# First batch's opening and last batch's end in another order: ranking, weight splits, maxima, and the split of the heads

## The reference

```python
def _L0_ffn_ref(x, w_router, w_block):
    k = max(1, int(L * CAPACITY_RATIO))            # 768 of 1024
    scores = jnp.einsum('bld,d->bl', x, w_router)
    _, top_idx = jax.lax.top_k(scores, k)
    selected = jnp.take_along_axis(x, top_idx[:, :, None], axis=1)
    processed = jax.nn.gelu(jnp.einsum('bkd,de->bke', selected, w_block))
    out = x.at[batch_idx, top_idx].set(processed)

def _L0_attn_ref(hidden_states, Wq, Wk_down, Wv_down, q_to_latent, v_up, Wout):
    Q = (hidden_states @ Wq.T).reshape(b, t, h, d)     # 16 heads of 32
    latent_k = hidden_states @ Wk_down.T               # 64 wide
    latent_v = hidden_states @ Wv_down.T
    q_lat = jnp.einsum('bthd,hdl->bthl', Q, q_to_latent)
    logits = jnp.einsum('bthl,bsl->bhts', q_lat, latent_k) / math.sqrt(l)
    # causal mask, softmax
    ctx_lat = jnp.einsum('bhts,bsl->bhtl', attn, latent_v)
    heads = jnp.einsum('bhtl,hld->bthd', ctx_lat, v_up)
    out = heads.reshape(b, t, h * d) @ Wout.T

x = x + 0.5 * _L0_ffn_ref(_layernorm(x), ...)
x = x + _L0_attn_ref(_layernorm(x), ...)
x = x + 0.5 * _L0_ffn_ref(_layernorm(x), ...)
```

## Time and profile before

| | us |
|---|---|
| median of three executions | 2589.89 |
| the profiled execution, its time | 2591.08 |
| the profiled execution, its span | 2589.4 |
| PE busy | 2348.7 (91%) |
| DVE busy | 1719.9 (66%) |
| ACT busy | 1181.7 (46%) |
| POOL busy | 395.1 (15%) |
| mean granted PE clock | 0.965 of full |

### The profile page before, as it was taken

The page is one execution under the profiler, slowest core; times in us unless marked ns, Lnnn a source line. Parts: engine busy times, 40 slices in busy tenths (PEclk is TensorE's granted clock), DMA queues, the critical chain, the costliest instruction groups (busy, mean ns, idle before and its releaser), DMA issues.

```text
span 2589.4 us, 53629 instructions
## 1 busy us (share of the span) xinstructions
PE 2348.7 (91%) x21888; PEld 1457.0 (56%) x21888; DVE 1719.9 (66%) x4806; ACT 1181.7 (46%) x2071; POOL 395.1 (15%) x510
## 2 busy tenths in 40 slices
PE   6769999899989998899998999989999899998976
PEld 4534567445664556645575546654476545674445
DVE  4658656785667756686566865678656785567735
ACT  3325543464425643356433554445543455424542
POOL 0101211112101121111111101111111112101121
PEclk9879999999999999999999999999999899999998
DMA  3200021100201002010111101210021100301000
GB/s 122 98 2 2 2 85 47 66 2 8 92 34 66 3 18 82 33 67 2 35 64 50 51 2 66 66 66 3 2 83 49 66 2 2 98 1 67 2 1 33
DMA packets 70034, 106.20 MB, mean 41 GB/s; under 512 B 3104, under 2 KB 33312, under 8 KB 67744
## 3 DMA queue, kind: packets, MB, share of 16 engines
q1 hardware_dynamic: 69792, 102.77, 11.6%
HBM read 64.49 MB, written 37.75 MB: 39 GB/s over the span
## 4 chain that ended last, share of the span: by engine, by line
PE 69%; DVE 12%; issue 10%; ACT 6%; POOL 2%; DMA 0%; DVEq 0%; POOLq 0%; ACTq 0%
PE psum L722 25%; PE psum L735 18%; PE psum L841 9%; PE psum L848 7%; PE psum L738 4%; DVE psum L973 4%; ACT pr L703 4%; PE psum L764 3%; PE psum L749 3%; DVE part L971 2%; DVE junk L923 1%; POOL rstd L596 1%; DVE junk L921 1%; DVE qk L960 1%; DVE nt_l L909 1%
## 5 line engine op out<-in xcount | busy, mean ns | idle before, releaser
L703 ACT ACTIVATE pr<-psum 128x512 f32<-128x512 f32 x1152 | 617.6, 597 | 621.3 <-PE psum L738 621.1
L735 PE MATMUL psum<-qk,qk 32*128 32x512 f32 (+3 forms) x4608 | 511.4, 369 | 97.8 <-ACT pr L703 38.9
L973 DVE CUSTOM_DVE_ANT_0 psum<-psum,mask_b 128x512 f32<-128x512 f32 (+3 forms) x1024 | 473.1, 522 | 166.6 <-PE psum L749 165.1
L735 PEld LDWEIGHTS psum<-qk,qk 32*128 32x128 f32 x4608 | 320.6, 186 | 402.9 <-ACT pr L703 123.0
L749 PE MATMUL psum<-qk,qk 32*128 32x512 f32 (+3 forms) x4608 | 514.1, 373 | 29.1 <-DVE part L971 19.6
L971 DVE TENSOR_REDUCE part<-psum 128x1 f32<-128x512 f32 x512 | 325.2, 681 | 71.7 <-PE psum L749 69.9
L749 PEld LDWEIGHTS psum<-qk,qk 32*128 32x128 f32 x4608 | 312.7, 189 | 57.5 <-DVE part L971 26.1
L614 POOL TENSOR_SCALAR_AFFINE_SELECT pr<-pr 128x512 f32<-128x512 f32 x256 | 158.0, 635 | 1056.6 <-ACT pr L703 1056.6
L841 PE MATMUL psum<-pr,v_sb 128*32 128x512 f32 (+3 forms) x3072 | 312.4, 502 | 1.6 <-ACT acc_sb L622 1.6
L848 PE MATMUL psum<-pr,ones 128*32 128x512 f32 (+3 forms) x3072 | 306.1, 493 | 0.0
L643 ACT ACTIVATE norm<-x,nmr,rstd 128x512 f32<-128x512 f32 x192 | 152.4, 810 | 193.4 <-DVE nmr L903 193.4
(11 more groups left out here) (115 smaller groups left out, 3411.4 us busy)
## 6 DMA issues: line engine op xcount, KB each, us to landing
x<-x_dram SPq DMA_DIRECT2D x16, 1024.0 KB, 6.8
spill_x<-x SPq DMA_DIRECT2D x16, 1024.0 KB, 5.2
x<-spill_x SPq DMA_DIRECT2D x16, 1024.0 KB, 7.7
out_dram<-x SPq DMA_DIRECT2D x16, 1024.0 KB, 5.1
w_h<-scratch_o SPq DMA_DIRECT2D x28, 256.0 KB, 3.1
w_l<-scratch_o SPq DMA_DIRECT2D x28, 256.0 KB, 3.3
w_h<-scratch_q SPq DMA_DIRECT2D x6, 1024.0 KB, 4.9
w_l<-scratch_q SPq DMA_DIRECT2D x6, 1024.0 KB, 6.9
```

Source lines behind the costliest of these rows:

```text
L703: nc.scalar.activation(pr_of(b, g, u)[:, 2 * p + place, :], bank(e, place), ACT.Exp, scale=SCALE).then_inc(exp_ready, 1)
L735: eng.matmul(o, (k_h, k_h, k_l)[t][own, P * j:P * (j + 1)], (q_h, q_l, q_h)[t][own, queries], start=(t == 0 and at == 0), stop=False, skip ...
L973: m = nc.vector.tensor_tensor_reduce(scores, scores, mask_b[:, BANK - w:BANK], 1.0, FAR, ALU.add, ALU.max, top_of)
```

## The change

In the first batch, `opening` replaces `front(0)`, `project(0, None)` and the maxima units 5 to 8 behind it. The first score product stands behind transposes 4 and 5; the splits 2, 3, 4 follow the second score's copy, and SCOL follows them; the first four layers stand in the list together with the ranking, then RF and all GX, then the other layers with the additions; split 5 comes ahead of the third addition. K of group 0 directly follows LAT. Maxima unit 7 stands ahead of the second LAT, and the others each stand ahead of one or two projections. All nine units of group 0 of the first batch take their banks from ring H.

In the last batch, `closing` replaces the `HS` list, `back(7)` and `ending(7)`. The heads of groups 0 to 2 are split inside group 3 (units 2 to 7), under waits of their own; those of group 3 when each half is ready, the second half of the tokens first. O, norms, transposes and scores run with the second half first. Two layers instead of four come before the ranking, and six behind it. Each half of the result is written in two pieces.

```diff
-    def front(b):
+    def opening():
...
         for i in range(NT):
-            out += [("T", 0, b, i)] + ([("NO", 0, b, i + 2)] if i + 2 < NT else [])
-            out += [("SC", 0, b, i // TC)] if i % TC == TC - 1 else []
-            out += [("WS", 1)] if i == TC else []
+            out += [("T", 0, 0, i)] + ([("NO", 0, 0, i + 2)] if i + 2 < NT else [])
+            out += [("SC", 0, 0, 0), ("WS", 1)] if i == 5 else []
+        out += [("SC", 0, 0, 1), ("WS", 2), ("WS", 3), ("WS", 4), ("SCOL", 0, 0)]
+        for i in range(TC):
+            out += layer(0, 0, i) + [("RT", 0, 0, 2 * i), ("RT", 0, 0, 2 * i + 1)]
+        out += [("RF", 0, 0)] + [("GX", 0, 0, i) for i in range(NT)]
+        out += layer(0, 0, 4) + layer(0, 0, 5) + summed(0, 0) + summed(0, 1) + [("WS", 5)]
+        out += layer(0, 0, 6) + summed(0, 2) + summed(0, 3) + scales(1, 0, 0) + layer(0, 0, 7) + [("NO", 1, 0, 0), ("NO", 1, 0, 1)]
+        after = [summed(0, 4), summed(0, 5), summed(0, 6), summed(0, 7) + scales(1, 0, 1)]
+        for i in range(TC):
+            out += [("T", 1, 0, i)] + ([("NO", 1, 0, i + 2)] if i + 2 < TC else []) + after[i]
+        out += [("LAT", 0, 0), ("XS", 0, 0), ("NO", 1, 0, 4), ("NO", 1, 0, 5), ("K", 0, 0, 0)]
+        out += [("Q", 0, 0, 0), ("T", 1, 0, 4), ("NO", 1, 0, 6), ("T", 1, 0, 5), ("NO", 1, 0, 7)]
+        out += [("Q", 0, 1, 0), ("T", 1, 0, 6), ("T", 1, 0, 7)] + maxima(0, 0, 7) + [("LAT", 0, 1), ("XS", 0, 1)]
+        out += [("XL", 1, 0), ("XL", 1, 1), ("K", 0, 0, 1), ("Q", 0, 0, 1)]
+        beside = [[("Q", 0, 1, 1)], [("K", 0, 1, 0), ("K", 0, 1, 1)], [("V", 0, 0), ("V", 0, 1)], [("Q", 0, 2, 0)],
+                  [("Q", 0, 2, 1)], [("Q", 0, 3, 0)], [("Q", 0, 3, 1)], [("V", 0, 2), ("V", 0, 3), ("V", 0, 4)]]
+        for u, rest in zip((0, 1, 2, 3, 4, 5, 6, 8), beside):
+            out += maxima(0, 0, u) + rest + sum([gathered(0, 0, c) for c in range(NC) if LAST[c] == u], [])
+            out += turned(0, 0, 1) if u == 8 else []
+        out += [("V", 0, 5), ("V", 0, 6), ("V", 0, 7), ("K", 0, 2, 0), ("K", 0, 2, 1)] + turned(0, 0, 0)
+        return out + [("K", 0, 3, 0), ("K", 0, 3, 1)]
...
-        if b + 1 == B:
-            out += layer(1, b, 6) + layer(1, b, 7)
+        return out
+
+    def closing(b, left):
+        out = left[0] + [("HS", b, NQ - 1, 1)] + left[1] + left[2] + left[3] + [("HS", b, NQ - 1, 0)]
+
+        def added(i):
+            return [("O", b, i)] + stats(2, b, i)
+
+        def turn(i):
+            after = (i + 2) % NT
+            return [("T", 2, b, i)] + ([("NO", 2, b, after)] if i % TC < 2 else [])
+
+        for i in range(TC, NT):
+            out += added(i)
+        out += scales(2, b, 1) + [("NO", 2, b, 4), ("NO", 2, b, 5)]
+        for i in range(TC):
+            out += added(i) + turn(TC + i)
+        out += scales(2, b, 0) + [("SC", 1, b, 1), ("NO", 2, b, 0), ("NO", 2, b, 1)] + layer(1, b, 4)
+        for i in range(TC):
+            out += turn(i)
+        out += [("SC", 1, b, 0)] + layer(1, b, 5) + [("SCOL", 1, b)] + [("RT", 1, b, i) for i in range(NT)] + [("RF", 1, b)]
+        order = (4, 5, 6, 7, 0, 1, 2, 3)
+        out += [("GX", 1, b, i) for i in order]
+        for i in (6, 7, 0, 1, 2, 3):
+            out += layer(1, b, i)
+        for i in order:
+            out += [("CB", 1, b, i)] + ([("OUT", b, i // TC)] if i % TC == TC - 1 else [])
         return out
...
+        else:
+            for n, (g, c) in enumerate((g, 1 - c) for g in range(NQ - 1) for c in range(NC)):
+                groups[NQ - 1][2 * n + 5] += [("HS", b, g, c)]
...
-            early = k == "MX" and e[2] == 0 and e[3] <= 4
+            early = k == "MX" and e[2] == 0 and (e[3] <= 4 or e[1] == 0)
...
+                    if b + 1 == B:
+                        sp.wait_ge(x1_ready, x1_nth["CB", 1, b, TC * c + 1])
+                        eng.dma_start(out[b, rows(c), :].rearrange("(i p) e -> p i e", p=P)[:, 0:2, :],
+                                      x1[:, TC * c:TC * c + 2, :]).then_inc(x_out[c], 16)
...
-                    act.wait_ge(heads_ready, nth["HE", b, NQ - 1, 0])
-                    act.wait_ge(q_done, nth["Q", min(b + 1, B - 1), NQ - 1, c])
+                    if b + 1 < B:
+                        act.wait_ge(heads_ready, nth["HE", b, NQ - 1, 0])
+                        act.wait_ge(q_done, nth["Q", b + 1, NQ - 1, c])
+                    else:
+                        act.wait_ge(heads_ready, nth["HE", b, g, c])
+                        act.wait_ge(s_done, nth["S", b, 1, UNITS - 1, 1])
```

More of the change, by code:

```diff
@@ L128, in summed @@
         return [("CB", 0, b, i)] + stats(1, b, i)
+    def opening():
+        out = []
+        for c in range(NC):
+            for i in range(TC * c, TC * (c + 1)):
+                out += stats(0, 0, i)
+            out += scales(0, 0, c)
+        out += [("WS", 0), ("NO", 0, 0, 0), ("NO", 0, 0, 1)]
+        for i in range(NT):
+            out += [("T", 0, 0, i)] + ([("NO", 0, 0, i + 2)] if i + 2 < NT else [])
[20 more added lines that the diff above has]
+        return out + [("K", 0, 3, 0), ("K", 0, 3, 1)]
@@ L130, in project @@
     def project(b, left):
[L134 to L137, removed]
+        out = [("G", 0, b, 0), ("G", 0, b, 1)]
         out += layer(0, b, 2) + layer(0, b, 3) + summed(b, 0) + summed(b, 1)
-        out += layer(0, b, 4) + summed(b, 2) + summed(b, 3) + scales(1, b, 0) + ([] if b else [("WS", 5)])
+        out += layer(0, b, 4) + summed(b, 2) + summed(b, 3) + scales(1, b, 0)
@@ L143, in project @@
         for i in range(TC):
[L144 removed]
+            out += [("T", 1, b, i)] + ([("NO", 1, b, i + 2)] if i + 2 < TC else []) + left[i] + after[i]
         out += [("LAT", b, 0), ("XS", b, 0), ("NO", 1, b, 4), ("NO", 1, b, 5)]
@@ L216, in more @@
         def more(kind, *rest):
-            return kind(b + 1, 0, *rest) if b + 1 < B else []
+            return kind(b + 1, 0, *rest)
         def turn(i):
@@ L242, in ending @@
         return out
-    sched = [("XL", 0, 0), ("XL", 0, 1)] + front(0) + project(0, None)
-    for u in range(5, UNITS):
-        sched += maxima(0, 0, u) + sum([gathered(0, 0, c) + turned(0, 0, c) for c in range(NC) if LAST[c] == u], [])
+    sched = [("XL", 0, 0), ("XL", 0, 1)] + opening()
     for b in range(B):
@@ L275, in program_order @@
         else:
-            sched += sum(left, []) + [("HS", b, g, c) for c in range(NC) for g in range(NQ)] + back(b) + sum(ending(b), [])
+            sched += closing(b, left)
     beside, taken = {}, set()
@@ L664, in _ @@
                     if f == 1:
-                        act.wait_ge(hsl_ready, nth["HS", b, NQ - 1, NC - 1])
+                        act.wait_ge(hsl_ready, max(nth["HS", b, NQ - 1, c] for c in range(NC)))
                     act.wait_ge(f_done, nth["F", f, b, i])
@@ L773, in _ @@
                     f, b = e[1:]
-                    pe.wait_ge(srow_ready, nth["SC", f, b, 1])
+                    pe.wait_ge(srow_ready, max(nth["SC", f, b, c] for c in range(NC)))
                     for i in range(NT):
@@ L916, in _ @@
                     dve.wait_ge(scol_ready, nth["SCOL", f, b])
-                    dve.wait_ge(srow_ready, nth["SC", f, b, NC - 1])
+                    dve.wait_ge(srow_ready, max(nth["SC", f, b, c] for c in range(NC)))
                     settled()
```

23 lines of the change are left out of this document (9 added, 14 removed).

## The result

The kernel after takes 2571.91 us (median of four executions, 2570.70 to 2573.86), the kernel before 2590.06 (four, 2589.05 to 2590.61): ratio 0.9931, 95% interval 0.9914 to 0.9948. That is 18.2 us less where 30.7 were forecast, and 0.9 us above the upper end of the range. The profiled execution took 2570.7, its span is 2568.9. It was the fastest of its four, and the profiled one of the kernel before (2591.08) lies above the median there, so the two spans differ by 20.5 us, not 18.2.

The account below looks back on a forecast made before the run. DVE's ranking and draining of maxima were taken to bound the time before the first scores, PE the attention. Opening 19.0 plus closing 11.7 gave 30.7 us less, so 2559.2 us against the median 2589.89; range 2549 to 2571.

Parts of the forecast that it names:

- (a): Opening, first score product behind transposes 4 and 5: the second score's copy, at 36.30, comes some 1.4 us earlier.
- (b): Opening, splits 2 to 4 straight behind that copy: ranking starts at 42.7 instead of 49.5, 6.8 us gained.
- (c): Opening, split 5 ahead of the third addition: first norm delayed 2.3 us plus 0.5 beside POOL; latent product at 78.2.
- (d): Latent product to first scores: PE's work 52 us plus some 9.5 of waits, so first scores at 139.7.
- (e): First batch's scores at full clock, exponentials 2.13 us apart: seventh at 153.8, opening gains 19.0 us.
- (f): Last group, six of eight head splits moved in: nothing on the path; 3 us if the cover is gone.
- (g): Last batch, seventh split and Wout: Wout starts at 2501.3 instead of 2508.93; four products end 10.2 us earlier.
- (h): Last batch, fourth addition to ranking: 36.5 us instead of 37.0, 0.5 gained, with 1.9 for low clock.
- (i): Last batch, ranking to end: stays 29.6 us except a last write half as large, 1.0 less.
- Rival 1: Opening's maxima on the H ring run serially: 12.5 us lost over five long units, time 2571; chance 0.12.
- Rival 3: First batch's attention runs at PE's low clock: 0.73 us per half unit, 53 for all, 2612; chance 0.03.

Follow-up runs that it names:

- warm: Kernel after, with 36 matmuls whose results nobody reads placed in PE's waits in the opening: 2572.68 us, ratio 0.9924.
- best2: Kernel after with K behind Q and unread matmuls in the waits of the opening, batch borders and last batch: 2551.04 us, ratio 0.9849.
- end_warm: Kernel after, with five unread matmuls ahead of the last norms' transpose 2 and five ahead of the second score product: 2571.36 us, ratio 0.9926.
- best: Kernel after with K behind Q, short projections spread among the maxima, unread matmuls at batch borders and in some opening waits: 2554.48 us, ratio 0.9857.
- k_behind_q: Kernel after, with K of group 0 behind Q in both halves instead of straight behind the latent product: 2565.39 us, ratio 0.9901.
- after_mid: Kernel after, with unread matmuls at two places of each of the seven batch borders: 2560.09 us, ratio 0.9883.

## Why the prediction was wrong, point by point

**(a), (b), (c) right.** Ranking, first addition and norm came 1.0 to 1.3 us ahead of the forecast, the latent product at 77.85 (78.2). Split 5 took 2.80 us beside POOL's tiles against 2.28 alone, the 0.5 that the forecast took. The Trainium skill ("SBUF — State Buffer", "Who interferes with whom") has the two exclude each other; the trace agrees, and POOL pays most of it. POOL's timeline, window 61.3 to 64.2:

```profile
61.12 3.30 POOL L653 TENSOR_SCALAR x<-x,gain,shift 128x512 f32<-128x512 f32 x1
```

That tile took 3.30 us where the first one took 0.77, and the eight together 9.96 instead of 7.98. As (c) said, nobody was waiting for the late ones.

**(d) failed, in its term "PE's work 52 us".** The first scores started at 146.34, not 139.7. From the latent product it was 68.5 us against 61.5. Of the 7.0, half clock behind three short waits is 4.7, by what the same work takes in `warm`. The waits as a whole are 0.2. The other 2.1 are the terms for full clock, which were too small: K with Q takes 3.9 even there (I had 3.5), a Q alone mostly 2.96 (I had 2.8). I had counted half clock for the first LAT alone, though I had four waits of 1.4 in the same sum. The rows I used could have warned me: the low clock of 130 to 140 stands beside a PE that works 3.53 us of 10.

That the waits came out right was luck. The terms of my list, 4 x 1.4 + 1.6 + 2.4 + 1.5, add up to 11.1 and not to the 9.5 in the sum. Measured were three waits of 1.50 and not four, 0.92 for T7, 1.83 for the maxima, and 1.01 + 1.46 at the end. With 11.1 the seventh exponential would have been put at 155.4, still 10.3 us early. Nor do the bounds of the terms give the range's lower end: the best bounds of (d) and of the closing, 22 and 15, lead to 2553 and not to 2549.

**(e) failed in "PE comes to them at full clock".** The clock fell as the scores began. The first exponential came 2.0 us behind the first scores (1.3 in the sum, and 1.3 in `warm`), and the six steps took 17.4 instead of 12.8. The two waits ahead, 1.01 and 1.46, brought it on: with them filled, `warm` and `best2` took 13.7 for the six steps. The forecast had the second of them; the first, K's bank held by the turning of the maxima, was missed. Together: 7.0 + 0.7 + 4.6 less 0.35 for the earlier start = 11.9, which is the gap between 19.0 and 7.1.

**(f), (g) right.** ACT in the last group of the kernel after, then DVE behind it:

```profile
2477.65 2.06 ACT L760 ACTIVATE pr<-psum 128x512 f32<-128x512 f32 x4 [0.84 <-PE psum L795]
2479.57 0.65 ACT L674 ACTIVATE nt_h<-ht 128x512 fp32r<-128x512 f32 x1
2481.09 2.07 ACT L760 ACTIVATE pr<-psum 128x512 f32<-128x512 f32 x4 [0.87 <-PE psum L795]
```

```profile
2491.89 0.72 DVE L1050 STREAM_TRANSPOSE rden<-psum 128x512 f32<-128x512 f32 x1 [3.29 <-PE psum L905]
...
2504.16 0.69 DVE L1066 TENSOR_TENSOR x<-psum,x 128x512 f32<-128x512 f32 x1 [1.38 <-PE psum L779]
...
2540.97 1.28 DVE L980 TENSOR_SCALAR_CACHE_REDUCE junk<-srow,scol 128x1024 bf16<-128x1024 f32 x1
```

The copy of the heads takes 0.65 and ACT still idles 0.87 ahead of the next scores. Wout starts at 2492.66, as DVE frees its bank; the fourth addition is 18.64 us earlier than the earlier trace rows, of which 8.67 are the shift of the group (2493.37 to 2484.70 in the windows at the top): 10.0 (forecast 10.2).

**(h) slightly high, (i) slightly low.** Fourth addition to ranking took 36.8 (36.5): 0.2 gained instead of 0.5. The waits were as counted: 1.55 (1.6), 1.75 (1.8), and 2.43 + 0.56 + 1.50 = 4.5 (4.5). The half clock behind them cost 1.3 (`end_warm`), I had taken 1.9; about 1.0 of the 36.8 is neither wait nor half clock and was not traced. Ranking to end went from 29.6 to 27.9, 1.7 gained against 1.0; four writes of 512 KB now land in 2.8 us (median).

**The rivals.** Rival 1 named the right size (2571) by the wrong mechanism: long waits for maxima between products exist on ring N only. Rival 3's mechanism, scores at low clock, was there for the same six half units as before, and for no later one of the first batch; I had put it down as unlikely instead of as six half units at 0.73, 4.4 us of the sum. Its argument that "every later batch runs at full clock" was wrong: the middle of the kernel before has 85 us at half clock, in 16 stretches of 3 to 7 us. The borders of the batches, forecast at nothing, gave 1.6 back here; in `warm` the middle is 9.2 us longer than in the kernel after. Why the time at half clock there moves between 75 and 92 us with nothing changed in the middle is open; the runs show only that it moves with the opening and from one execution to the next, and that filling the waits halves it. Even with them filled the middles of `best` and `best2` differ by 7.3 us.

## What to carry to other kernels

Where PE's timeline shows waits of a microsecond or more in a row of short products, price each as its own length and, as an upper bound, the products behind it at half clock: 3.9 us of waits removed were worth 8.3, but several waits of the same length cost only themselves. Order the list so that a product stands between an operand's split and its use, and give pairs that take four banks a ring of eight. What is left can be filled with matmuls nobody reads; behind a wait that still pulls the clock down they cost time (`best`). Judge an opening by the whole time, since the borders behind it can take the gain back.

## What the runs showed of the hardware beyond that

- Short waits can pull the granted clock down: 1.50 us at 84 and 100 and 1.02 at 118 were each followed by windows at 0.50 to 0.54, while 1.50 at 107 was not, nor was 1.03 in `k_behind_q`. What tells the two apart is open. The Trainium skill ("TensorE: Matmul & The Clock Gate", "A second HAM failure mode: psum-queue depth-cycling") tells of a kernel whose short and frequent idling makes the clock swing between its two levels; the trace agrees, and filling the waits of the opening (`warm`) brought 8.0 us.
- The same scores, waiting for ACT in the same way, ran at either level: PE busy for 1.20 of 2 us at 1.00 in `warm` (148 to 150), and for 1.22 of 2 at 0.50 in the kernel after (148 to 150). The level at the first score does not decide alone: in `best` PE began at half clock, ran at 1.00 in 146 to 148 and at 0.50 again in 148 to 150. With the waits ahead filled, `warm` kept 1.00 for 8 us of scores, then fell for 3.4.
- Matmuls that nobody reads can pay where PE waits. `after_mid` runs 168 of them and is 11.8 us faster than the kernel after; the 36 of `warm` brought 8.0 us by the seventh exponential and nothing in the total.
- A DVE subtraction with both inputs in SBUF took 2.80 us beside POOL's tiles (2.28 without), and the POOL tile that it met took 3.30 us against 0.77.
